# A decoder kernel on one core: GpSimd pauses at the router and the exact norm, rows transposed between the last z transposes, the mixture norm's first half early, key copies between its roots

## What is computed

```
x = x + L0_attn(norm(x))          # delta rule, exact decays: softplus of x @ W_alpha
x = x + L0_xattn(norm(x), ctx)    # 16 heads, tanh layers for q, k, v
x = x + L0_ffn(norm(x))           # router, top 2 of 4 experts, norm of hidden rows, norm of the mixture
x = x + L1_attn(norm(x))          # latent q, k, v, causal
x = x + L1_xattn(norm(x), ctx)    # causal over the context
x = x + L1_ffn(norm(x))           # 8 experts, top 2, gelu
```

## Time and profile before

| | |
|---|---|
| median of 3 runs | 6094.07 us (6084.75 to 6096.39) |
| profiled execution | 6093.98 us, span 6092.2 us |
| mean granted clock of TensorE | 0.931 |
| TensorE matmul, busy | 5011.9 us (82%) |
| VectorE | 4276.4 us (70%) |
| GpSimd | 3844.2 us (63%) |
| ScalarE | 2280.3 us (37%) |
| chain that ended last | PE 56%, DVE 23%, issue 9%, ACT 7%, POOL 3% |

### The profile page before, as it was taken

How to read it: one execution, slowest core, us unless ns; L and a number is a source line. 1 busy time by engine, 2 the same in 40 slices (tenths; PEclk the granted TensorE clock), 3 DMA queues, 4 the chain that set the end, 5 groups by cost and what they waited for, 6 DMA issues and landing times.

```text
span 6092.2 us, 107412 instructions
## 1 busy us (share of the span) xinstructions
PE 5011.9 (82%) x28914; PEld 3244.2 (53%) x28914; DVE 4276.4 (70%) x11906; ACT 2280.3 (37%) x4416; POOL 3844.2 (63%) x10626
## 2 busy tenths in 40 slices
PE   0088888888888888888888888888888888888888
PEld 0055655546565564656546565554656556465654
DVE  5867676766767667676866767676676767767686
ACT  0043433443343444433343443344334344443334
POOL 1068475765847567485766847576584756758475
PEclk9599999999999999999999999999999999999999
DMA  3000000000000000000000000000000000000000
GB/s 86 2 10 8 19 1 22 5 8 19 8 19 1 22 5 8 19 8 19 1 12 15 8 19 1 22 5 8 19 8 19 1 23 5 8 19 8 12 1 15
DMA packets 61969, 79.06 MB, mean 13 GB/s; under 512 B 11168, under 2 KB 53808, under 8 KB 61232
## 3 DMA queue, kind: packets, MB, share of 16 engines
q1 hardware_dynamic: 52784, 62.42, 3.1%
q10 hardware_dynamic: 8448, 8.39, 0.4%
HBM read 45.04 MB, written 8.46 MB: 9 GB/s over the span
## 4 chain that ended last, share of the span: by engine, by line
PE 56%; DVE 23%; issue 9%; ACT 7%; POOL 3%; DMA 1%; SPq 1%; DVEq 0%; POOLq 0%; ACTq 0%
PE bank L1017 6%; PE bank L1112 6%; PE bank L1031 6%; PE bank L1041 4%; PE bank L1143 4%; PE bank L941 3%; PE bank L840 3%; PE bank L1063 3%; PE bank L948 2%; PE bank L1023 2%; PE bank L1050 2%; POOL arena L557 2%; ACT arena L742 1%; DVE arena L1824 1%; PE bank L897 1%
## 5 line engine op out<-in xcount | busy, mean ns | idle before, releaser
L1691 DVE TENSOR_REDUCE smax<-bank 128x4 f32<-128x512 f32 x768 | 524.9, 684 | 172.4 <-PE bank L1023 129.8
L725 ACT ACTIVATE arena<-bank 128x512 f32<-128x512 f32 x768 | 456.1, 594 | 468.1 <-PE bank L1031 466.0
L718 ACT ACTIVATE arena<-arena 128x512 f32<-128x512 f32 x768 | 482.6, 628 | 215.9 <-DVE arena L1695 215.4
L1695 DVE TENSOR_TENSOR arena<-bank,smax 128x512 f32<-128x512 f32 x768 | 530.8, 691 | 26.4
L1031 PE MATMUL bank<-ident,arena 128*128 128x128 f32 x3072 | 498.3, 286 | 29.8 <-ACT arena L718 29.8
L1112 PE MATMUL bank<-w,arena 128*128 128x512 f32 x1024 | 503.7, 624 | 14.0 <-DVE arena L1635 14.0
L1017 PE MATMUL bank<-arena 64*128 64x512 f32 x1536 | 445.6, 657 | 65.0 <-DVE arena L1873 27.1
L1041 PE MATMUL bank<-arena 128*32 128x128 f32 x6144 | 333.0, 289 | 189.5 <-ACT arena L729 189.5
L557 POOL TENSOR_TENSOR arena<-arena,levmask 128x512 f32<-128x512 f32 x192 | 264.2, 1392 | 347.8 <-PE bank L941 224.9
L1031 PEld LDWEIGHTS bank<-ident,arena 128*128 128x128 f32 x3072 | 357.1, 144 | 227.3 <-ACT arena L718 115.7
L840 PE MATMUL bank<-causal,identb 128*128 128x512 bf16 x1266 | 320.5, 406 | 179.0 <-DVE y_nat L1483 167.4
(11 more groups left out here) (420 smaller groups left out, 12147.8 us busy)
## 6 DMA issues: line engine op xcount, KB each, us to landing
arena<-in_x_dram SPq DMA_DIRECT2D x35, 512.0 KB, 3.5
xn_next<-arena SPq DMA_DIRECT2D x17, 512.0 KB, 2.9
arena<-cum_dram SPq DMA_DIRECT2D x17, 512.0 KB, 3.5
arena<-in_ctx_dram SPq DMA_DIRECT2D x16, 512.0 KB, 3.6
out_dram<-arena ACTq DMA_DIRECT2D x16, 512.0 KB, 3.2
xn<-xn_next SPq DMA_DIRECT2D x15, 512.0 KB, 2.9
w<-in_L_ffn_w_dram SPq DMA_DIRECT2D x8, 512.0 KB
w<-in_L_ffn_w_dram SPq DMA_DIRECT2D x1, 1024.0 KB
```

What stands on the lines that cost most here:

```text
L718: act.activation(Ssb[:, v % 4], Ssb[:, v % 4], ACT.Exp, scale=SCALE).then_inc(S["p_exp"], 1)
L725: act.activation(PT[:, v % 2], bank[3 + v % 2][:, :].rearrange("p (h q) -> p h q", h=QH), ACT.Copy).then_inc(S["pt"], 1)
L1691: dve.tensor_reduce(smax[:, u, :], sc, AX, ALU.max).then_inc(S["s_max"], 1)
L1695: dve.tensor_tensor(Ssb[:, u % 4], sc, smax[:, u, :].unsqueeze(2).broadcast_to([P, QH, P]), ALU.subtract).then_inc(S["s_sub"], 1)
```

## The change

On GpSimd the list of work stays and its order moves. The links of slice 0 run to their end without waiting for `layer_norm(1)`; the products of slice 1 and four of its links follow; then the second bias addition; then GpSimd waits for the router's gates (`g_w`). After two links of slice 2 it waits for the exact norm (`x_norm`). On TensorE the transposes of the next rows leave `key_features` and stand behind the z transposes 1 and 2 of the last expert; `beta_columns` writes bank 3 instead of 7 and no longer waits for `acc`; the fillers before `to_features(3)` are 16 instead of 20. ScalarE copies those rows right after the last expert, the keys between the two roots of the mixture norm, and takes the exponential of beta before the roots of `layer_norm(3)`. VectorE norms the first two tiles of the mixture before it sums the last two. The function `mixture_norm` itself stays word for word; it is only defined ahead of the experts' loop. The steps of `decay_exponential` leave the last four score steps of attention 2 and stand behind them.

```diff
                 pool.wait_ge(S["xn"], at(it, "xn", 4))
                 pool.tensor_tensor(xres[:, :, :], xres[:, :, :], bo_row[:, :].unsqueeze(1).broadcast_to([P, G, D]), ALU.add).then_inc(S["bias_res"], 1)
                 pool.wait_ge(ref_step, nth(it, REF_STEPS, REF_BEFORE + ROOT_STEPS))
-                chain_links(pool, link, 0, 0, 14)
+                chain_links(pool, link, 0, 0, 16)
+                chain_products(pool, link, src, 1)
+                chain_links(pool, link, 1, 0, 4)
 
                 pool.wait_ge(S["xn"], at(it, "xn", 8))
                 pool.tensor_tensor(xres[:, :, :], xres[:, :, :], onb_row[:, :].unsqueeze(1).broadcast_to([P, G, D]), ALU.add).then_inc(S["bias_res"], 1)
-                chain_links(pool, link, 0, 14, 16)
-                chain_products(pool, link, src, 1)
-                chain_links(pool, link, 1, 0, 8)
-                chain_links(pool, link, 1, 8, 16)
+                pool.wait_ge(S["g_w"], at(it, "g_w", 1))
+                chain_links(pool, link, 1, 4, 16)
                 chain_products(pool, link, src, 2)
-                chain_links(pool, link, 2, 0, 8)
-                chain_links(pool, link, 2, 8, 16)
+                chain_links(pool, link, 2, 0, 2)
+
+                pool.wait_ge(x_norm, nth(it, 1, 1, 2))
+                chain_links(pool, link, 2, 2, 16)
                 pool.wait_ge(S["xT_dve"], at(it, "xT_dve", 4))
                 chain_products(pool, link, src, 3)
...
                     act.activation(rkT[:, h, :, 1:P + 1], heads(bank[4 + h][:, :]), ACT.Copy).then_inc(S["rkT"], 1)
+
+            def row_copies(it, a):
+
                 for c in range(C):
...
-
-                    for m in range(2):
+                def half_rstd(s, first=0, last=2):
+
+                    for m in range(first, last):
...
-                half_rstd(2)
+                row_copies(it, 1)
+                half_rstd(2, 0, 1)
                 key_copies(it, 1)
+                half_rstd(2, 1, 2)
+                beta_exp(it, 1)
 
 
                 half_rstd(3)
-                beta_exp(it, 1)
...
-            def key_features(it, a, src):
+            def row_features(c, src):
+
+                for g in range(G):
+                    ins = tr(bank[2 + c][:, g * P:(g + 1) * P], src[:, g, c * P:(c + 1) * P], ident[:, :])
+                ins.then_inc(S["ax_psum"], 1)
+
+            def key_features(it, a):
 
                 pe.wait_ge(S["rk"], nth(it, 1, 1, a))
...
                     ins.then_inc(S["rk_psum"], 1)
-                for c in range(C):
-                    for g in range(G):
-                        ins = tr(bank[2 + c][:, g * P:(g + 1) * P], src[:, g, c * P:(c + 1) * P], ident[:, :])
-                    ins.then_inc(S["ax_psum"], 1)
...
-                        ins = mm(bank[7][:, g * DH:(g + 1) * DH], xT[:, c, g * P:(g + 1) * P], Wab[:, c, :], start=(c == 0), stop=(c == C - 1))
+                        ins = mm(bank[3][:, g * DH:(g + 1) * DH], xT[:, c, g * P:(g + 1) * P], Wab[:, c, :], start=(c == 0), stop=(c == C - 1))
...
-            key_features(0, 0, xn0)
+            pe.wait_ge(moved_now, 16)
+            for c in range(C):
+                row_features(c, xn0)
+            key_features(0, 0)
...
                         if e + 1 < E0:
                             up(e + 1, k)
+                        elif k in (1, 2):
+                            row_features(k - 1, xn_next)
...
-                key_features(it, 1, xn_next)
-                pe.wait_ge(S["acc"], at(it, "acc", 16))
+                key_features(it, 1)
                 beta_columns(it, 1)
-                keep_busy(20, 2)
+                keep_busy(MIX_FILL, 2)
...
                                 wait("t_psum", base + u - 3)
                             dve.tensor_tensor(Ssb[:, u % 4], sc, smax[:, u, :].unsqueeze(2).broadcast_to([P, QH, P]), ALU.subtract).then_inc(S["s_sub"], 1)
-                            if a_no == 2 and u >= 12:
-                                decay_exponential(u - 12)
                         if u >= 6 and (u - 6) % 4 == 3 and (u - 6) // 4 < G:
                             b = (u - 6) // 4
-                            if a_no == 2 and b == 2:
-                                decay_exponential(4)
-                                decay_exponential(5)
-                                decay_exponential(6)
-                            if a_no == 2 and b == 3:
-                                decay_exponential(7)
-                                decay_exponential(8)
-                                decay_exponential(9)
+                            if a_no == 2 and b >= 2:
+                                for part in range(5 * (b - 2), 5 * (b - 1)):
+                                    decay_exponential(part)
                             wait("otr_psum", a_no * G + b + 1)
                             o = bank[7][:, :].rearrange("p (h d) -> p h d", d=2 * HD)
...
                             if e == E0 and g % 2:
                                 wait("acc", 12 + g + 1)
                                 half_stats(2, g // 2, acc)
+                                if g == 1:
+                                    mixture_norm(0)
...
-                layer_norm(3, xres, mixture_norm)
+                layer_norm(3, xres, lambda m: mixture_norm(m) if m else None)
...
+MIX_FILL = 16
```

More of the change, by code:

```diff
@@ L646, in beta_exp @@
                 act.wait_ge(S["ab_psum"], nth(it, 1, 1, a))
-                act.activation(col[:, :, :].rearrange("p g h -> p (g h)"), bank[7][:, 0:G * DH], ACT.Exp, scale=-1.0).then_inc(S["beta_exp"], 1)
+                act.activation(col[:, :, :].rearrange("p g h -> p (g h)"), bank[3][:, 0:G * DH], ACT.Exp, scale=-1.0).then_inc(S["beta_exp"], 1)
             def decay_exp(it, a):
@@ L659, in _ @@
             key_scale(0, 0)
+            row_copies(0, 0)
             key_copies(0, 0)
@@ L670, in ln_rstd @@
                     act.activation(rstd[:, :], lnv[:, :], ACT.Exp, scale=-0.5).then_inc(S["ln_rstd"], 1)
-                def half_rstd(s):
-                    for m in range(2):
+                def half_rstd(s, first=0, last=2):
+                    for m in range(first, last):
                         two = slice(2 * m, 2 * m + 2)
@@ L1812, in router, with mixture_norm @@
                     wait("g_w", 1)
+                def mixture_norm(m):
+                    half_root(2, m)
+                    for g in (2 * m, 2 * m + 1):
+                        dve.scalar_tensor_tensor(out=acc[:, g, :], in0=acc[:, g, :], scalar=mv[:, g, 0:1], in1=ong_row[:, :], op0=ALU.subtract, op1=ALU.mult).then_inc(S["moe_g"], 1)
+                    wait("bias_res", 2)
+                    for g in (2 * m, 2 * m + 1):
+                        wait("moe_g", g + 1)
+                        ins = dve.scalar_tensor_tensor(out=xres[:, g, :], in0=acc[:, g, :], scalar=rstd[:, g:g + 1], in1=xres[:, g, :], op0=ALU.mult, op1=ALU.add)
+                    ins.then_inc(S["res"], 1)
+                    wait("res", 4 + m + 1)
                 for e in range(E0 + 1):
@@ L1850, in _ @@
                         exact_norm(1)
-                def mixture_norm(m):
-                    half_root(2, m)
-                    for g in (2 * m, 2 * m + 1):
-                        dve.scalar_tensor_tensor(out=acc[:, g, :], in0=acc[:, g, :], scalar=mv[:, g, 0:1], in1=ong_row[:, :], op0=ALU.subtract, op1=ALU.mult).then_inc(S["moe_g"], 1)
-                    wait("bias_res", 2)
-                    for g in (2 * m, 2 * m + 1):
-                        wait("moe_g", g + 1)
-                        ins = dve.scalar_tensor_tensor(out=xres[:, g, :], in0=acc[:, g, :], scalar=rstd[:, g:g + 1], in1=xres[:, g, :], op0=ALU.mult, op1=ALU.add)
-                    ins.then_inc(S["res"], 1)
-                    wait("res", 4 + m + 1)
-                layer_norm(3, xres, mixture_norm)
+                layer_norm(3, xres, lambda m: mixture_norm(m) if m else None)
                 xT_copy(3)
```

## The result

The changed kernel takes 6106.09 us (median of 9 runs, 6104.39 to 6108.18), the kernel before on the same chip 6089.26 (9 runs): a ratio of 1.0027, 95% interval 1.0016 to 1.0037. I had forecast 6044. So it came out slower, where I had given 0.18 to slower; it lies just inside my range of 8 in 10 (to 6108). The profiled execution of the changed kernel has a span of 6106.4 us against 6092.2.

The account below looks back on a forecast made before the run. No engine bounds a pass alone: TensorE, VectorE and ScalarE hand work to each other. Terms -2.2 -2.8 +0.4 -2.0 +3.5 = -3.1 us a pass, -50 us in sixteen: 6044 us, likeliest 6025 to 6065, 8 in 10 5980 to 6108.

Parts of the forecast that it names:

- small steps: Layer norm 1: eight small VectorE steps beside GpSimd's products take 0.21 us more each, +1.7 us a pass.
- row writes L1631: Layer norm 1: four row writes counted at nothing beside products; by the skill's rule up to 2.0 us more.
- statistics' steps: Before the router: three statistics steps now lie beside links instead of products, -0.8 us.
- router itself: Router: first part undelayed beside links, then GpSimd's 2.35 us addition in its way; gates -2.2 us net of earlier terms.
- gates to exact norm: Experts: TensorE's dry stretch shrinks from 4.2 to about 1.2 us, so its clock stays up, -2.8 us.
- rows to latT: Behind layer norm 3: closing the gap before the transposes gives -2.0 us, matmuls at 1.2 GHz cost +3.5.
- Layer norm 1 ... +1.7: Layer norm 1 gets GpSimd's products beside it; its small steps cost +1.7 us, ends 0 and +3.4.
- slower rival: Products stretch layer norm 1, TensorE cools, up projections at 1.2 GHz cost +3.4; +1.8 us a pass, 6123 us; chance 0.18.
- The gain at the exact norm: After the experts: the exact norm starts 5.0 us earlier.
- The exact norm's pause: GpSimd's second pause is reached after its event and holds nobody: 0 gain, ends 0 and -2.5 us.
- The mixture's first half: Mixture norm: first half brought forward, but VectorE waits for ScalarE's Ln and Exp without other work, +0.4 us.
- Decay steps: Steps moved from attention's last score steps to before the reciprocals: 0 us, ends -0.4 and +0.4.

Follow-up runs that it names:

- e7: The changed kernel with 26 instead of 14 fillers before layer norm 1's transposes; 0.9976 of the kernel before, 0.5% below the changed kernel.
- e2: The changed kernel with ScalarE's exponential for the gates behind the first z copy instead of the second; 1.0014 of the kernel before.
- e1: The changed kernel, but slice 1's products wait for layer norm 1, and bias addition and all slice 1 links for the gates; 0.9886 of the kernel before.
- e3: The kernel before with the mixture's edits alone, GpSimd's order and decay steps as before; 1.0089 of the kernel before.
- e6: The kernel before with GpSimd's new order and the moved decay steps, mixture's stage as before; 1.0020 of the kernel before.
- e9: e6 with slice 1's products held until layer norm 1 has written its rows, GpSimd ordered as in e1; 0.9928 of the kernel before.
- e4: The changed kernel with 56 instead of 16 fillers before layer norm 3's transposes; 0.9934 of the kernel before, 0.9% below the changed kernel.
- e5: The changed kernel with the edits of e1 and e4 together; 0.9873 of the kernel before.
- e10: e5 with e2's edit, the gates' exponential behind the first z copy; 0.9862 of the kernel before.

## Why the prediction was wrong, step by step

| from, to | forecast | measured |
|---|---|---|
| addition to router: small steps | +1.7 | +1.5 |
| row writes L1631 | 0 | +1.6 |
| TensorE's clock in the first projections | 0 | +2.9 |
| statistics' steps | -0.8 | -0.7 |
| router itself | -3.1 | -2.8 |
| gates to exact norm | -2.8 | -2.5 |
| exact norm to rows of layer norm 3 | +0.4 | +0.4 |
| rows to latT | +1.5 | +0.3 |
| pass | -3.1 | +0.7 |

(Statistics' steps: what is left of the measured +5.3.)

**The step that failed** is "Layer norm 1 ... +1.7": it should have been +6.0, and this 4.3 is more than the whole error. Two terms were missing. I counted the row writes at nothing since no row showed them beside products; the trace has 1.6: each write, 0.41 us alone, takes 0.70 to 0.88 and ends only behind the end of a product. An absent row was not a zero. By the rule of the Trainium skill (SBUF — State Buffer, Who interferes with whom) my estimate for them was up to 2.0 us; with 1.6 us and every write held until a product has ended, the trace agrees. And the longer norm leaves TensorE dry before the transposes, which lowers its clock for the first projections. That was the slower rival's mechanism, in the main: it had all eight small steps waiting, where half of them and the writes did. Its price for the projections, 3.4, was measured at 2.9 here and 2.8 in e7's two kinds of passes. I gave it 0.18 because half of the small steps don't wait, and left out of the count the writes that all do. The norm was 9.7 us long (I had written that it decides from about 9.5).

**The router** was right in size and wrong in mechanism: the addition L585 was not met, since the router started 4 us later than forecast; a wait for ScalarE's queue of 3.28 us took its place. e2 takes most of this wait away, and the second expert's transposes stay where they were: TensorE's cold projections were behind it.

**The gain at the exact norm** (5.0) came to 0: gates 2.5 late instead of 2.2 early, while the clock at the experts gave 2.5 of its 2.8. With layer norm 1 free it is 7.0 (e1).

**The exact norm's pause** held nobody and gained nothing, as forecast: products of slice 2 lay on the block, and one pair of L1378 still took 1.82 us. **The mixture's first half** was right (+0.4). **From the rows to latT** I had +1.5 and it was +0.3: the gap gave 1.5 instead of 2.0, and the cold matmuls cost 1.8 instead of 3.5, since L1172 and L1174, which I had counted, were at the full clock. **Decay steps**: 0, as forecast, so far as the means of the rest of a pass tell. `au` came 4 us earlier, not 10, since GpSimd's new pause at the gates is 10.75 us, nearly the 12.87 it saved at L583.

**What the stage of the mixture is worth** is not settled: its edits are +0.9% with the old order (e3), +0.1% or nothing with the new (changed kernel against e6), -0.4% with e1's order (against e9). VectorE's steps themselves differ by 1.5 us at most; the rest goes with TensorE's clock at the latent matmuls, L1172 and L1174 above all (at 1.2 GHz in 11 of 16 passes in e3, 15 in e9, 9 in e1, none in the changed kernel). What decides that from pass to pass, with TensorE's work the same to 0.1 us (e7: 5.13 and 5.25 of 7.20 us busy before the two outcomes; e4: 0.4 us idle before both), I did not settle. It is luck as far as these runs go, and part of the changed kernel's +0.3% can be such luck. Nor did I try a change that makes only the row writes immune to the products.

## What to carry to other kernels

When work of GpSimd is moved, price every VectorE instruction beside its new place, the large SBUF-to-SBUF ones above all, and where no row shows the pair, take a bound and not zero; then ask whether a stretch that grows by 3 us leaves TensorE dry and its clock falls, for here that doubled the price. The better version lets GpSimd stand during the norm (e1, e5, e10: 1.1 to 1.4% below the kernel before), since its idle time cost nothing there, and its busy time beside VectorE did.

## What the runs showed of the hardware that I had not expected

- A VectorE `TENSOR_SCALAR` with two operands per row, 128x256 f32 from SBUF to SBUF, takes 0.41 us alone and 0.70 to 0.88 beside GpSimd's 128x256 products of 0.73, and ends 0.15 us after the end of a product.
- One GpSimd instruction of 2.35 us on a 128x1024 tile makes four 128x4 VectorE instructions take 2.60 us instead of 0.62 (e7); one of them takes 2.20.
- The same kernel has passes with the clock at 1.00 and at 0.54 in the same stretch, 4 us apart (e7). The idle time before the next work does not decide alone: with 40 more fillers and 0.4 us idle the clock held at the latent matmuls in twelve passes and fell in four (e4: 1.96 and 3.1 to 3.2 us for four); with 1.07 to 1.56 us idle it fell in all sixteen (e5: 3.0 to 3.75 us).
